# An audio tower on one core: where the dense experts' weights are loaded and split, and where the attention weights' scales are made

## The reference

```python
scores = softmax(xt @ gate_w + gate_b)          # groups of 2, best 4 groups, best 4 experts
up = silu(einsum('td,edh->teh', xt, Wu) + bu)   # 16 experts, D 192, hidden 128
gt = einsum('td,edh->teh', xt, Wg) + bg
y = einsum('teh,ehd->td', up * gt * w_full[:, :, None], Wd) + w_full @ bd
y = y + (silu(xt @ sWu + sbu) * (xt @ sWg + sbg)) @ sWd + sbd
```

## Time and profile before

| | |
|---|---|
| median of 3 runs | 4266.16 (4258.59 to 4273.0) |
| the profiled execution, time | 4268.25 |
| its span | 4266.6 |
| PE busy | 3479.6 (82%) |
| DVE busy | 3403.5 (80%) |
| ACT busy | 2599.5 (61%) |
| POOL busy | 1847.7 (43%) |
| clock granted to TensorE, mean | 0.865 |

### The profile page before, as it was taken

The page is one execution under the profiler, slowest core; times in us unless marked ns, Lnnn a source line. Parts: engine busy times, 40 slices in busy tenths (PEclk is TensorE's granted clock), DMA queues, the critical chain, the costliest instruction groups (busy, mean ns, idle before and its releaser), DMA issues. The chain is left out here.

```text
span 4266.6 us, 68495 instructions
## 1 busy us (share of the span) xinstructions
PE 3479.6 (82%) x22579; PEld 2669.3 (63%) x22628; DVE 3403.5 (80%) x6255; ACT 2599.5 (61%) x5081; POOL 1847.7 (43%) x2264
## 2 busy tenths in 40 slices
PE   0049999999489999999999777888868887456998
PEld 0039999999479999999999652111112222445998
DVE  7949888889667777777777677999988887785886
ACT  4735555555234444444444468999989998453665
POOL 5757777777323333333334101222222110464665
PEclk9999999999789999999999666555558999557999
DMA  4334445554422122212222139100011111237996
GB/s 116 105 85 138 137 137 142 143 145 138 115 88 76 63 94 94 95 68 74 94 91 88 51 110 358 30 25 25 25 42 36 54 50 43 80 115 205 273 269 176
DMA packets 288617, 458.27 MB, mean 107 GB/s; under 512 B 45619, under 2 KB 223362, under 8 KB 277374
## 3 DMA queue, kind: packets, MB, share of 16 engines
q1 hardware_dynamic: 268350, 428.16, 32.8%
q0 software_dynamic: 18944, 25.85, 2.1%
q10 hardware_dynamic: 1024, 0.54, 0.0%
HBM read 355.23 MB, written 105.12 MB: 108 GB/s over the span
## 5 line engine op out<-in xcount | busy, mean ns | idle before, releaser
L1101 POOL TENSOR_TENSOR c_ap<-c_ac,c_ap 128x420 fp32r<-128x420 f32 x340 | 406.4, 1195 | 761.6 <-ACT c_ap L1260 761.5
L726 PE MATMUL b_pA<-ab_woutT,b_ys 128*105 128x192 f32 x3840 | 689.5, 326 | 1.2 <-ACT b_ho L646 0.4
L726 PEld LDWEIGHTS b_pA<-ab_woutT,b_ys 128*105 128x105 f32 x3840 | 610.6, 171 | 12.1 <-ACT b_ho L646 3.9
L564 POOL TENSOR_TENSOR b_ys<-b_hs,b_cb 128x525 f32<-128x525 f32 x384 | 507.0, 1321 | 221.9 <-DVE b_hs L791 179.8
L1947 DVE TENSOR_REDUCE g_raw<-g_pS 128x1 f32<-128x525 f32 x816 | 549.6, 703 | 31.4 <-PE g_pS L1902 30.1
L1923 ACT ACTIVATE g_pS<-g_pS,g_stt 128x525 f32<-128x525 f32 x816 | 553.7, 776 | 19.8 <-POOL g_stt L1876 19.0
L1902 PE MATMUL g_pS<-g_qk 16*128 16x262 bf16 (+1 forms) x1536 | 461.5, 408 | 94.2 <-ACT g_pS L1923 34.8
L1260 ACT ACTIVATE c_ap<-c_ac 128x420 fp32r<-128x420 f32 x340 | 189.3, 557 | 554.0 <-DVE c_ac L1427 552.3
L791 DVE TENSOR_TENSOR_SCAN b_hs<-b_ae,b_pB 128x525 f32<-128x525 f32 x384 | 479.3, 1248 | 41.2 <-ACT b_ae L665 7.3
L1169 PE MATMUL c_pD<-cw_wd,c_ap 128*105 128x192 f32 x4080 | 439.3, 257 | 27.1 <-POOL c_ap L1101 27.1
L1169 PEld LDWEIGHTS c_pD<-cw_wd,c_ap 128*105 128x105 f32 x4080 | 424.7, 172 | 51.5 <-POOL c_ap L1101 38.6
(11 more groups left out here) (417 smaller groups left out, 7671.7 us busy)
## 6 DMA issues: line engine op xcount, KB each, us to landing
b_cb<-dram_ct SPq DMA_DIRECT2D x64, 1050.0 KB
c_wb<-dram_wt SPq DMA_DIRECT2D x60, 840.0 KB, 9.7
b_cb<-dram_ct SPq DMA_DIRECT2D x64, 525.0 KB
dram_slots<-g_empty SPq DMA_DIRECT2D x33, 772.0 KB, 20.2
c_wb<-dram_wt SPq DMA_DIRECT2D x20, 1050.0 KB, 6.4
m_wo_r<-in_L_ffn_wo_dram SPq DMA_DIRECT2D x24, 576.0 KB
o_wo_r<-in_L_ffn_wo_dram SPq DMA_DIRECT2D x24, 576.0 KB
dram_qk<-f_qk SPq DMA_DIRECT2D x16, 787.5 KB
```

What stands on the lines that cost most here:

```text
L564: pool.tensor_tensor(ys[:, u % RING, :], hs[:, u % RING, :], cb[:, g % 3, u % GU, :], ALU.mult).then_inc(s["ys"], 1)
L726: ins = pe.matmul(into, ys[:, u % RING, t * TP:(t + 1) * TP], woutT[:, u % NU, :], start=(u == 0 and t % 2 == 0), stop=(u % NU == NU - 1), ...
L1101: nc.gpsimd.tensor_tensor(ap[LO][:, r, :], ac[:, r, :], ap[HI][:, r, :].bitcast(F32), ALU.subtract)\
```

## The change

The first four raw tensors of the dense experts get a place of their own in SBUF (`cw_spare`) that is held from the start of the kernel. SP issues their loads within the last two batches of the scan: Wu's six DMAs ahead of `b_cb` group 2 of batch 14, Wg's six ahead of group 0 of batch 15. The weights block is gone. Its work stands in the dense experts' block: ACT makes the high parts 0 to 3 first of all and the high part 4 after `exps(0)`; the low parts 0, 1 and 4 are POOL's, 2 and 3 are DVE's. The raw Wd loads into the space of raw 2 and 3 when their low parts are done. The buffer `wb` lies in the same space. The attention weights load after the first rows; their maxima stand before `route` 0 on DVE, their scaling, rounding and copies after statistics 1, ahead of `hidden(0, 0, 0)`. PE waits for all of that before the loop. To make room, `junk` and `junk_a` become rings of two, with waits to match.

```diff
...
-        junk, junk_a = sb("junk", [P, G, N_IN], BF16), sb("junk_a", [P, G, N_IN], BF16)
+        junk, junk_a = sb("junk", [P, 2, N_IN], BF16), sb("junk_a", [P, 2, N_IN], BF16)
...
+                    if b * G + g >= 2:
+                        act.wait_ge(s_sign, b * G + g - 1)
+                    act.activation(junk_a[:, g % 2, :], srow[:, slot, :], ACT.Sign, bias=nsc[:, slot, g:g + 1],
...
+                    if b * G + g >= 2:
+                        dve.wait_ge(s_tie, b * G + g - 1)
+                    v.scalar_tensor_tensor(junk[:, g % 2, :], srow[:, slot, :], sc[:, slot, g:g + 1], order[:, g, :],
...
+    LATER_AT = ({2: 0}, {0: 1})
...
+                    if not load and g in LATER_AT[k]:
+                        load_later(sp, LATER_AT[k][g])
...
-def dense_experts(nc, h1, gate_w, gate_b, bias, wu, bu, wg, bg, wd, bd, swu, sbu, swg, sbg, swd, sbd, wt_d, h2,
+def dense_loads(nc, keep, wu, wg, swu, swg):
+
+    E, HID, KA, KB = 16, 128, 128, D - 128
+    EA = E + 1
+    spare = keep.enter_context(nc.sbuf_tensor("cw_spare", [128, 13 * 4 * TP + EA * D], F32))
+    raw = [spare[:, n * EA * HID:(n + 1) * EA * HID].rearrange("p (e n) -> p e n", e=EA) for n in range(4)]
+    sem = semaphores(nc, keep, "cw_")
+    s_raw = [sem(f"s_raw{n}") for n in range(5)]
+    early = {"spare": spare, "raw": raw, "s_raw": s_raw}
+
+    def load(sp, part):
+        we, ws = ((wu, swu), (wg, swg))[part]
+        sp.dma_start(raw[part][:, 0:E, :], we[:, 0:KA, :].rearrange("e p n -> p e n")).then_inc(s_raw[part], 16)
+        sp.dma_start(raw[part][:, E, :], ws[0:KA, :]).then_inc(s_raw[part], 16)
+        for r in range(2):
+            into = raw[2 + part][r * KB:(r + 1) * KB, :, :]
+            sp.dma_start(into[:, 0:E, :], we[:, KA:D, :].rearrange("e p n -> p e n")).then_inc(s_raw[2 + part], 16)
+            sp.dma_start(into[:, E, :], ws[KA:D, :]).then_inc(s_raw[2 + part], 16)
+
+    early["load"] = load
+    return early
...
+    spare = early["spare"]
+    wb = spare[:, 0:EA * N].rearrange("p (e n) -> p e n", e=EA)
+    raws = [early["raw"][0], early["raw"][1], early["raw"][2], early["raw"][3],
+            spare[:, GROUPS[3][0] * N:GROUPS[3][0] * N + EA * D].rearrange("p (e n) -> p e n", e=EA)]
...
+        pDQ, pF = ps("pD", [128, 2, 512]), ps("pF", [128, 512])
+        pD, pQ = pDQ[0:TP, :, :], pDQ[:, :, :].bitcast(BF16)
+        later = z[0:KC, :, :, :].rearrange("p k t d -> p (k t) d")
+        wq_n, wp_n = later[:, 0:6, :], later[:, 6:8, :]
...
+        def low_part(eng, n):
+            eng.wait_ge(s_hi, n + 1)
+            p = slice(KB, 2 * KB) if n in (2, 3) else slice(0, 128)
+            eng.tensor_tensor(lows[n][p, :, :], raws[n][p, :, :], highs[n][p, :, :].bitcast(F32), ALU.subtract).then_inc(s_lo[n], 1)
...
                 sp.dma_start(h[:, c, :, :], tiles(h1, c)).then_inc(s_h[c], 16)
+            sp.dma_start(wq_n[:, :, :], w_qkv.rearrange("(r p) c -> p r c", p=KC)).then_inc(s_wq, 16)
+            sp.dma_start(wp_n[:, :, :], w_proj.rearrange("(r p) c -> p r c", p=KC)).then_inc(s_wq, 16)
...
-            weights(0, range(len(GROUPS)))
+            sp.dma_start(K["bv"][:, :], row(b_qkv[2 * D:3 * D]).broadcast_to([TP, D])).then_inc(s_bq, 16)
+            sp.wait_ge(s_k0, 6)
...
+            for n in (2, 3):
+                sp.wait_ge(s_lo[n], 1)
+            sp.dma_start(raws[4][:, 0:E, :], wd.rearrange("e p n -> p e n")).then_inc(s_raw[4], 16)
+            sp.dma_start(raws[4][:, E, :], swd).then_inc(s_raw[4], 16)
+            for n in (0, 1):
+                sp.wait_ge(s_lo[n], 1)
+            weights(0, range(3))
+            sp.wait_ge(s_lo[4], 1)
+            weights(0, (3,))
             rows(2)
...
+            pool.memset(K["amax"][:, :], 0.0).then_inc(s_k0, 1)
+            pool.memset(K["ident"][:, :], 0.0).then_inc(s_k0, 1)
+            pool.memset(K["wT"][:, :, :], 0.0).then_inc(s_k0, 1)
...
+            low_part(pool, 0)
+            low_part(pool, 1)
...
                 x_low(0, 0, cc)
+            pool.wait_ge(s_wm, 2)
+            pool.partition_all_reduce(K["gmax"][:, 1:3], K["amax"][:, 1:3], 128, bass.bass_isa.ReduceOp.max)\
+                .then_inc(s_wall, 1)
+            low_part(pool, 4)
...
+            pe.wait_ge(s_id, 2)
+            for step in range(2):
+                front_pe(0, 0, 0, step)
             pe.wait_ge(s_w, N_W)
-            pe.wait_ge(s_id, 2)
+            for step in range(2, FS - 1):
+                front_pe(0, 0, 0, step)
+            pe.wait_ge(s["wT"], at(0, 1, 1))
             for n in range(2):
                 ins = pe.transpose(pF[:, n * EA:(n + 1) * EA], bn[:, n, :], ident[0:EA, 0:EA])
             ins.then_inc(s_bn, 1)
-            pe.wait_ge(s_bc, 1)
-            for step in range(FS - 1):
-                front_pe(0, 0, 0, step)
+            for n in range(4):
+                pe.wait_ge(s_lo[n], 1)
...
             up_gate(0, 0, 0)
+            pe.wait_ge(s_tc, 1)
+            pe.wait_ge(s_k, 1)
+            for c in range(KT):
+                for r in range(6):
+                    ins = pe.transpose(pQ[0:KC, c, r * KC:(r + 1) * KC], wq_b[:, r, c * KC:(c + 1) * KC],
+                                       K["ident"][0:KC, 0:KC])
+                ins.then_inc(s_t, 1)
+            pe.wait_ge(s_tc, 2)
+            wp = wp_b[:, :, :, :].rearrange("p r h d -> p r (h d)")
+            for g in range(HG):
+                for r in range(2):
+                    ins = pe.transpose(pQ[:, 0, g * D + r * KC:g * D + (r + 1) * KC], wp[:, r, g * 128:(g + 1) * 128],
+                                       K["ident"][0:KC, 0:KC])
+            ins.then_inc(s_t, 1)
+            pe.wait_ge(s_bc, 1)
+            pe.wait_ge(s_tc, 3)
+            pe.wait_ge(s_lo[4], 1)
...
+            def high_part(n):
+                act.wait_ge(s_raw[n], 64 if n in (2, 3) else 32)
+                act.activation(highs[n][:, :, :], raws[n][:, :, :], ACT.Copy).then_inc(s_hi, 1)
+
+            for n in range(4):
+                high_part(n)
             for t in range(CT):
                 normalise(0, 0, t)
             for step in range(2):
                 front_act(0, 0, 0, step)
             x_high(0, 0)
             exps(0)
+            high_part(4)
             front_act(0, 0, 0, 3)
+            act.wait_ge(s_bn, 1)
+            act.activation(bc[:, :, :], pF[:, 0:2 * EA].rearrange("p (n e) -> p n e", n=2), ACT.Copy)\
+                .then_inc(s_bc, 1)
+            act.wait_ge(s_bc, 1)
...
-            dve.wait_ge(s_w, N_W)
-            dve.wait_ge(s_id, 2)
             st = Steps(dve, s_va, VP, 0)
             for part in range(4):
                 statistics(0, 0, 0, part, st)
+            low_part(dve, 2)
+            low_part(dve, 3)
+            dve.wait_ge(s_k0, 6)
+            dve.wait_ge(s_wq, 32)
...
+            dve.wait_ge(s_w, N_W)
+            dve.wait_ge(s_id, 2)
             st = Steps(dve, s_ro, RP, 0)
             for part in range(11):
                 route(0, 0, part, st)
...
             for part in range(4):
                 statistics(1, 0, 1, part, st)
+            st = Steps(dve, s_v2)
+            dve.wait_ge(s_wall, 1)
+            quant_scale(nc, st, K["sc"][:, 1:3], K["inv"][:, 1:3], K["gmax"][:, 1:3])
+            st.counted(v.tensor_scalar(wq_n[:, :, :], wq_n[:, :, :], K["inv"][0:KC, 1:2], MAGIC, ALU.mult, ALU.add))
+            st.after(v.tensor_scalar(wp_n[:, :, :], wp_n[:, :, :], K["inv"][0:KC, 2:3], MAGIC, ALU.mult, ALU.add))
+            st.counted(v.tensor_scalar(wq_b[:, :, :], wq_n[:, :, :], -MAGIC, None, ALU.add))
+            for r in range(2):
+                ins = v.tensor_scalar(wp_b[:, r, :, 0:HD], wp_n[:, r, :].rearrange("p (h d) -> p h d", d=HD),
+                                      -MAGIC, None, ALU.add)
+            st.after(ins)
+            dve.sem_inc(s_tc, 1)
+            for c in range(KT):
+                dve.wait_ge(s_t, c + 1)
+                for r in range(4):
...
+            ins.then_inc(s_tc, 1)
+            dve.wait_ge(s_t, 3)
+            for g in range(HG):
+                ins = v.tensor_copy(K["wpT"][:, g, :], pQ[:, 0, g * D:(g + 1) * D])
+            ins.then_inc(s_tc, 1)
...
+    with ExitStack() as lasting:
+        K = attention_constants(nc, lasting)
+        dense_held = ExitStack()
+        early = dense_loads(nc, dense_held, wu, wg, swu, swg)
+        with ExitStack() as held:
+            W = scan_constants(nc, held)
+            token_selection(nc, x, tok_gamma, tok_beta, tok_w, tok_b, dram("score", (NB, N_IN)), h0,
+                            ssm_lam, ssm_wd, ssm_bd, ssm_wb, ssm_wc, ssm_wout, ssm_bout, W)
+            ssm(nc, h0, W, dram("ct", (NB, 16, S)), h1, early["load"])
+        dense_experts(nc, early, dense_held, h1, gate_w, gate_b, gate_bias, wu, bu, wg, bg, wd, bd, swu, sbu, swg, sbg, swd, sbd,
...
```

172 lines of the change are left out of this document (33 added, 139 removed).

## The result

| | before | after |
|---|---|---|
| median of 7 runs each | 4266.16 (4255.81 to 4273.0) | 4241.94 (4236.75 to 4258.99) |
| ratio after / before, 95% interval | | 0.9952 (0.994 to 0.9964) |
| span of the profiled execution | 4266.6 | 4242.1 |
| first issue after the scan, s | 1121.19 | 1128.93 |
| the mark, start of `up_gate` 2 | 1200.03 (s + 78.8) | 1186.72 (s + 57.8) |

The forecast was 4246, from 4228 to 4258, faster with 0.76. The kernel is 24 us or 0.48% faster, and the whole interval lies beyond 0.3%.

What follows compares the result with a forecast made beforehand. Loading bounds the weights block after the scan, then a chain of latencies runs to the mark. 4266.6 - 20.6 (mark) + 1 (scan) + 0.6 (block end) - 2 (clock) = 4245.6, forecast 4246, range 4228 to 4258.

Steps and rivals of the forecast that it cites:

- one more end of a block: End of the dense experts: one more clearing and meeting costs 0.6 us (0 to 1.5).
- Steps 1 to 4: First chunk's preparation, from rows of h landing through POOL's low parts and the statistics to logits at s + 25.7.
- step 3: First chunk's statistics: POOL's long subtractions hold DVE's short instructions, costing 8.7 us; statistics ready at s + 17.1.
- uncovered value: First chunk's statistics without POOL's holds on DVE: ready at s + 7.7.
- Rival B: First chunk's preparation: POOL's long instructions hold DVE briefly or not at all; mark gains 36.2 us, time 4230; 20%.
- Step 5: `route`: 10.45 us to s + 36.2 uncovered, plus 6.9 held by POOL's low part 4; w at s + 43.1.
- step 6: After w: statistics 1 take 4.2 us, to s + 47.3; attention weights scaled by 50.1, turned and copied by 54.2.
- The scan's term: Last scan batch: coefficients land late behind the Wg loads, costing 1 us (0 to 6).
- POOL or DVE waiting over 3 us on `b_cb`: Scan batches 14 and 15: such a wait was to show that the early loads hurt the scan.
- rival D: Scan: raw loads move slower between the scan's own loads and delay batch 15; 4269 at 35 us; 4%.
- A: The forecast itself, first chunk's preparation with the holds as summed: 4246, by itself 4238 to 4254; 58%.
- The clock's term: PE behind the mark: `up_gate` 1 joins the unbroken run, shortening the half-clock time; gain 2 us (-1 to 4).

Runs made afterwards that it cites:

- e_dve_low: The changed kernel with POOL's three low parts (0, 1 and 4) given to DVE; median 4231.5 us, ratio to before 0.9935.
- e_low4_first: The changed kernel with POOL's low part 4 put ahead of its all-reduce instead of behind it; 4240.7 us in one run.
- e_again: The changed kernel run once more, unchanged, beside the kernel before; median 4241.6 us of 12 runs, ratio to before 0.997.
- e_part1_later: The changed kernel with the Wg loads issued ahead of the last scan batch's third coefficient group instead of its first; median 4236.2 us, ratio to before 0.993.

## Why the prediction was right, step by step

| step | forecast | measured |
|---|---|---|
| 1. rows of h landed | s + 3.5 | s + 3.4 |
| 2. POOL's low parts, 2176 and 3264 | 4.8, 7.1 | 4.78, 7.07 |
| 3. statistics ready, after two holds | 17.1 | 16.6 |
| 4. logits | 25.7 | 25.4 |
| 5. w | 43.1, `route` held | 35.9, not held |
| 6. statistics 1 ready | 47.3 | 46.9, held here |
| 7. mark | 58.2 | 57.8 |
| loss in the scan | 1 (0 to 6) | 7.7 (4.8 to 7.7 over six kernels) |
| clock behind the mark | 2 gained | 5.3 gained |
| one more end of a block | 0.6 | 0.6 |

The last line is the lead at the last result row (18.1) less that at the first load of the next stage, the attention inputs (17.5).

**Steps 1 to 4** were right to 0.5 us. What carried them was step 3: from an instruction of 0.17 us that took 1.06 beside a POOL instruction of 1.10 to holds of 4.7. e_dve_low shows that it is the cause: the forecast's uncovered value for the statistics was 7.7, and 7.7 was measured. By the Trainium skill, SBUF — State Buffer, section "Who interferes with whom", the lock is held for the whole instruction, whichever of the two engines took it first; the rows of 4.65, 4.69, 7.01 and 7.42 us on DVE, and of 3.72 on POOL, agree. Rival B, with short holds, is out.

**Step 5 failed, and step 6 made up for it.** The forecast let low part 4 start with its data and put its 6.9 on `route`. It overlooked POOL's idle time at the all-reduce, for which the kernel before has a row with 8.55 of "issue" ahead of it. Part of that was waiting for the maxima, but 4.7 us of it lie behind the end of the second of them:

```profile
1127.68 0.54 DVE L927 TENSOR_REDUCE k_amax<-d_wp_n 96x1 f32<-96x384 f32 x1
```

The 7 us fell behind w instead, on the same chain of DVE. e_low4_first built the case of the forecast, w 42.6 for 43.1, and the mark was the same. The sum was robust because it did not matter which instruction is held, only that DVE has no slack up to the mark.

**The scan's term was mis-sized.** The mechanism was named (the group of batch 15 lands late, POOL and then DVE wait) and its landing was nearly right: 16.1 after the first Wg issue (1057.34 to 1073.43, where POOL starts) in place of 15.8. Two things were not. DVE's ring of `hs` was full 15.2 after that issue (1074.86 less the 2.32 waited, less 1057.34), where the forecast had 17.3 (1055.60 to 1072.88). It had taken the wrong row: in the kernel before, the first unit of batch 15 reaches POOL at 1064.55 after the scan at 1063.17, so the scan four units on, the first that needs `ys` 0, is the one at 1070.94, 15.3 after the issue.

```profile
1064.55 1.30 POOL L564 TENSOR_TENSOR b_ys<-b_hs,b_cb 128x525 f32<-128x525 f32 x1 [0.69 <-DVE b_hs L791]
...
1070.94 1.25 DVE L791 TENSOR_TENSOR_SCAN b_hs<-b_ae,b_pB 128x525 f32<-128x525 f32 x1
```

With this row the forecast's own sum has DVE waiting 1.8 us, and 2.3 was measured. And the wait had a price behind it, of which the forecast had seen 1.07 in batch 0 and taken 1 for the whole: PE stood idle 4.33 us, came back at the lower clock, and DVE waited 3.6 us for it. Of the 7.7, 5.9 are these waits; the rest is the batch's start, 1.7 later in this execution (1057.34 against 1055.60), of which 0.6 was there at the scan's start. e_again, the same kernel, has it at 1057.1, and the nine others at 1054.8 to 1055.9; what this comes from isn't shown. e_part1_later takes the whole term away by one number.

**One sign was badly set.** The forecast named "POOL or DVE waiting over 3 us on `b_cb`" as the sign of rival D, with a loss in the scan that eats up the change. POOL waited 7.87, and D is still wrong: the group landed when the forecast had said. Its own sum had POOL free for the group from 1064.55 and the group there near 1071.4, a wait of 6.9. The sign could not tell A from D; DVE's wait could. Of its other signs, the two held instructions of the statistics and the mark came. A held instruction of `route` did not, nor a stretch of 40 to 45 us without matmuls: the longest there was 26.6, up to 1148.02.

**The clock's term** was undersized, 2 for 5.3. The forecast counted on the 4 us of `up_gate` 1 alone. In fact the lower clock ended before the mark, and all of the earlier trace rows's ten slow microseconds behind it went. The other merged kernels have 58.6 to 60.3 from the mark to the first result row, before has 64.1, so 3.8 to 5.5 is what it brings.

Together: 7.7 - 21.0 - 5.3 + 0.6 = -18.0 by the trace, where the forecast had -21.0. Two misses of opposite sign, +6.7 and -3.3, left 3.4, and the mark was 0.4 better. The medians differ by 24.2 here and by 20.6 in e_again's comparison; what the later stages add, 6.4 in the profiled execution and nothing clear in the medians, lies over all of them. The forecast owes some of its nearness to that and to its errors' signs.

## What to carry to other kernels

In these runs a subtraction moved from DVE to an "idle" POOL was not free for DVE: with both inputs in SBUF it held one of DVE's short instructions on tiles in SBUF for its whole length, 4.7 to 7.1 us each time. Before moving it, ask what DVE does in that time; here doing the work on DVE itself, at twice the speed, was 9 us faster. A load hidden in a stage cost by its place in the issuing queue (4.8 to 7.7 us, or none), not by its bytes: put it behind the transfer that is needed next. And where PE waits for a few microseconds in a full stage, count the slower clock after it as well as the wait.
